# Attention stage of a fused transformer block on one core: the product of the new tokens' values, from one fp32 pass to three fp32r passes with split operands

## The reference

```python
# one sequence: L = 512 cached positions, 32 new ones, 8 key heads, 4 query heads for each
k_all = concat([k_cache[block_table], k], axis=1)      # (544, 8, 128)
v_all = concat([v_cache[block_table], v], axis=1)
scores = einsum('qhd,khd->hqk', q, k_all) * SCALE      # masked behind cache_seqlens
probs = softmax(scores, axis=-1)
o = einsum('hqk,khd->qhd', probs, v_all)               # 512 cached + 32 new positions
out = einsum('se,de->sd', o, Wo)
```

## Time and profile before

| | |
|---|---|
| median of 3 runs | 1250.58 us (1247.67 to 1251.4) |
| profiled execution, its own time | 1247.98 us |
| its span | 1246.0 us |
| busy share of PE, DVE, ACT, POOL | 98%, 63%, 63%, 60% |
| attention of the first and second half | about 160 to 472 us and 780 to 1093 us |

### The profile page before, as it was taken

One profiled execution on the slowest core, in us unless ns is written; L12 is line 12 of the kernel. 1 busy time (PEld: TensorE's weight loads), 2 busy tenths in 40 slices (PEclk: granted clock), 3 DMA queues, 4 the chain that ended last, 5 costly groups with the idle time before them and its releaser, 6 DMA issues.

```text
span 1246.0 us, 28884 instructions
## 1 busy us (share of the span) xinstructions
PE 1221.7 (98%) x7378; PEld 1037.5 (83%) x7378; DVE 782.0 (63%) x1736; ACT 789.6 (63%) x2259; POOL 746.8 (60%) x884
## 2 busy tenths in 40 slices
PE   7999999999999999999999999999999999999998
PEld 6788889999999988865777888889999999988756
DVE  5976666666666668951459666666666666655422
ACT  5666678778877874432345766777887788644320
POOL 5344468888888885433233443788888888744320
PEclk9999999999999999999999999999999999999999
DMA  6524299999999955306135252899999999434300
GB/s 207 194 95 143 98 235 248 235 222 244 234 229 242 232 146 180 142 10 193 68 104 187 85 171 86 236 237 246 228 241 235 229 241 239 109 118 156 90 27 34
DMA packets 147978, 214.82 MB, mean 172 GB/s; under 512 B 24949, under 2 KB 119479, under 8 KB 142136
## 3 DMA queue, kind: packets, MB, share of 16 engines
q1 hardware_dynamic: 123480, 199.62, 58.9%
q10 hardware_dynamic: 24416, 14.28, 4.8%
HBM read 203.33 MB, written 10.49 MB: 172 GB/s over the span
## 4 chain that ended last, share of the span: by engine, by line
PE 91%; DVE 3%; ACT 2%; issue 2%; ACTq 1%; POOL 1%; DMA 0%; DVEq 0%; SPq 0%; POOLq 0%
PE PS L1157 18%; PE PS L1125 9%; PE PS L1224 5%; PE PS L1215 5%; PE PS L1019 5%; PE PS L1221 5%; PE PS L1023 5%; PE PS L1017 5%; PE PS L1167 4%; PE PS L1090 2%; PE PS L1266 2%; PE PS L1108 2%; PE PS L1092 2%; PE PS L1112 2%; PE PS L1102 2%
## 5 line engine op out<-in xcount | busy, mean ns | idle before, releaser
L628 POOL TENSOR_TENSOR kv_parts<-kv,k_hi 128x544 fp32r<-128x544 f32 x192 | 258.1, 1345 | 26.5 <-ACT k_hi L813 26.5
L1157 PE MATMUL PS<-probT,kv 128*128 128x128 f32 x2048 | 270.4, 275 | 0.0
L588 POOL TENSOR_TENSOR ring_parts<-ring,kv_parts 128x512 fp32r<-128x512 f32 x96 | 126.1, 1319 | 209.1 <-ACT kv_parts L691 180.5
L1654 DVE CUSTOM_DVE_ANT_0 ring<-PS,mask,rq 128x544 f32<-128x544 f32 x192 | 150.2, 782 | 158.3 <-PE PS L1113 97.2
L1157 PEld LDWEIGHTS PS<-probT,kv 128*128 128x128 f32 x2048 | 248.9, 192 | 0.0
L870 ACT ACTIVATE ring<-ring,smin 128x544 f32<-128x544 f32 x192 | 143.0, 745 | 97.1 <-DVE smin L1654 94.0
L1665 DVE COPY probT<-PS 128x512 f32<-128x512 f32 x256 | 172.1, 672 | 5.5 <-PE PS L1125 5.5
L650 POOL TENSOR_TENSOR ring_parts<-ring,kv_parts 128x512 fp32r<-128x512 f32 x64 | 84.9, 1330 | 95.3 <-ACT kv_parts L924 95.3
L813 ACT ACTIVATE k_hi<-kv 128x544 fp32r<-128x544 f32 x192 | 124.9, 652 | 16.2 <-DMA kv<-in_kpages 3.9
L616 POOL TENSOR_SCALAR ring<-ring,rinv 128x512 f32<-128x512 f32 x192 | 133.2, 694 | 0.0
L1692 DVE TENSOR_TENSOR qo_parts<-qo,kv_parts 128x512 fp32r<-128x512 f32 x64 | 85.3, 1339 | 54.2 <-ACT kv_parts L932 51.5
(11 more groups left out here) (217 smaller groups left out, 2718.6 us busy)
## 6 DMA issues: line engine op xcount, KB each, us to landing
kv<-in_kpages SPq DMA_DIRECT2D x512, 128.0 KB, 3.3
kv<-in_vpages SPq DMA_DIRECT2D x512, 128.0 KB
ring<-in_w SPq DMA_DIRECT2D x44, 1024.0 KB, 5.1
k_new<-kv ACTq DMA_DIRECT2D x16, 256.0 KB, 2.3
kv<-k_new ACTq DMA_DIRECT2D x28, 128.0 KB, 3.9
kv<-v_new ACTq DMA_DIRECT2D x28, 128.0 KB
kv<-in_xT SPq DMA_DIRECT2D x8, 256.0 KB, 5.3
ring<-in_w SPq DMA_DIRECT2D x8, 256.0 KB, 5.9
```

The source lines that it names most:

```text
L628: nc.gpsimd.tensor_tensor(kbuf_lo(par)[:, :, g, :], kbuf(par)[:, :, g, :], k_hi[:, e % 2, :].rearrange("p (j t) -> p j t", t=PSIZE), ALU.s ...
L1157: mm = nc.tensor.matmul(PS[:, at:at + D], vbuf(bpar)[:, c, gg * D:(gg + 1) * D], probT[:, g % 2, c * P:(c + 1) * P], start=(c == 0 and a = ...
L1654: V.tensor_tensor_reduce(prob(g % PRING)[:, 0:LK], PS[:, at:at + LK], mask[:, par, :], rq[:, par, g:g + 1], 3.0e38, ALU.add, ALU.min, smin ...
```

## The change

`values_new` no longer multiplies `vnew` with `spread` in fp32, but `vnew_hi x spread_hi`, `vnew_lo x spread_hi` and `vnew_hi x spread_lo`, three fp32r matmuls of 512 columns. For that:

- ScalarE's four copies now write fp32r (`spread_hi`), and ScalarE also makes `vnew_hi`, once for each sequence, in its step 4 (5 in the first sequence).
- VectorE makes `spread_lo` with four subtractions of 32x128 (`lower_spread`) at the end of its steps 3 and 7; the third pass and the next turn of new probabilities wait for it.
- GpSimd makes `vnew_lo` (`lower_values`, 128x256) in its step 7, and its low parts of keys move: those of heads 0 and 4 from steps 0 and 4 into the plain head's steps 7 and 3 before them, ahead of the scaling there.
- VectorE takes the reciprocal ahead of the mask instead of behind it in steps 0 and 4, those that follow the subtractions.
- `spread_lo` and `vnew_hi` are new storage, two areas are cleared instead of one.

```diff
-        KVSZ = 18944
+        KVSZ = 19968
...
+                def lower_values(b, par):
+                    pool.wait_ge(vhi_ready, h * HB + b + 1)
+                    nc.gpsimd.tensor_tensor(vnew_lo(par), vnew(par), vnew_hi(par), ALU.subtract).then_inc(vlo_ready, 1)
...
                 def lower_keys(b, par, first, last=False):
+                    if first:
+                        lower_key(b, par, 0)
                     for g in range(HK):
...
-                        if g % GU < NS:
-                            e = g // GU * NS + g % GU
-                            pool.wait_ge(khi_ready, (h * HB + b) * NSB + e + 1)
...
+                        if g % GU == NS and g < HK - 1:
+                            lower_key(b, par, g + 1)
+                        elif g == HK - 1:
+                            lower_values(b, par)
+                            if not last:
+                                lower_key(b + 1, 1 - par, 0)
+                        elif 0 < g % GU < NS:
+                            lower_key(b, par, g)
                         if g >= 2:
                             scale_probs(b, g - 2, first)
...
+                def upper_values(b, par):
...
+                        act.wait_ge(v_in[par], h * (n_in * HB // 2 - less) + (b - par) * (n_in // 2) + n_in - less)
...
+                    nc.scalar.activation(vnew_hi(par), vnew(par), ACT.Copy).then_inc(vhi_ready, 1)
...
+                    if g == (5 if first else 4):
+                        upper_values(b, par)
...
                 def values_new(b, par, u):
+                    if u == 0:
+                        pe.wait_ge(vlo_ready, h * HB + b + 1)
                     pe.wait_ge(spread_ready, GU * (h * QUADS + b * UNITS + u + 1))
-                    nc.tensor.matmul(bank(6 + u), vnew(par)[:, u * D:(u + 1) * D], spread, start=False, stop=True)\
-                        .then_inc(o_done, 1)
+                    nc.tensor.matmul(bank(6 + u), hi, spread_hi, start=False, stop=False)
+                    nc.tensor.matmul(bank(6 + u), lo, spread_hi, start=False, stop=False)
+                    pe.wait_ge(spread_low, GU * (h * QUADS + b * UNITS + u + 1))
+                    nc.tensor.matmul(bank(6 + u), hi, spread_lo, start=False, stop=True).then_inc(o_done, 1)
...
+                def lower_spread(b, u):
+                    dve.wait_ge(spread_ready, GU * (h * QUADS + b * UNITS + u + 1))
+                    for a in range(GU):
+                        rows = slice(a * SEQ, (a + 1) * SEQ)
+                        V.tensor_tensor(spread_lo[rows, a * P:(a + 1) * P], PS[rows, 2560:2688],
+                                        spread_hi[rows, a * P:(a + 1) * P], ALU.subtract).then_inc(spread_low, 1)
...
                 def step(b, par, g, first):
+                    early = g % GU == 0 and g < HK and not (first and g <= GU)
+                    if early:
+                        reciprocal(b, g)
...
-                    if g <= HK and not (first and g == 0):
-                        V.reciprocal(rinv[:, k:k + 1], rsum[:, k:k + 1]).then_inc(rinv_ready, 1)
+                    if g <= HK and not (first and g == 0) and not early:
+                        reciprocal(b, g)
...
+                    if g < HK and g % GU == 3 and not (first and g < GU):
+                        lower_spread(b if g > GU else b - 1, int(g < GU))
```

More of the change, by code:

```diff
@@ L201, in vnew, with vnew_hi, vnew_lo @@
             return kv[:, at:at + UNITS * D]
-        spread = kv[:, 2 * (KSZ + VSZ):2 * (KSZ + VSZ) + GU * P]
+        SP_HI, SP_LO, VN_HI = 2 * (KSZ + VSZ), 18944, 19456
+        spread_hi = kv_parts[:, SP_HI:SP_HI + GU * P]
+        spread_lo = kv_parts[:, SP_LO:SP_LO + GU * P]
+        def vnew_hi(u):
+            return kv_parts[:, VN_HI + u * UNITS * D:VN_HI + (u + 1) * UNITS * D]
+        def vnew_lo(u):
+            at = 2 * KSZ + u * VSZ + 4 * HK * D
+            return kv_parts[:, at:at + UNITS * D]
         junk = [prob0[:, 0:512], probT[:, :, :].rearrange("p a x -> p (a x)")[:, 512:1024]]
@@ L357, in build @@
         spread_ready = sem("spread_ready")
+        spread_low = sem("spread_low")
+        vhi_ready = sem("vhi_ready")
+        vlo_ready = sem("vlo_ready")
         o_done = sem("o_done")
@@ L825, in spread_new @@
                     if isinstance(b, int) and b == 0 and u == 0:
-                        act.wait_ge(spread_clear, h + 1)
+                        act.wait_ge(spread_clear, 2 * h + 2)
                     else:
@@ L831, in spread_new @@
                         rows = slice(a * SEQ, (a + 1) * SEQ)
-                        nc.scalar.activation(spread[rows, a * P:(a + 1) * P], PS[rows, 2560:2688], ACT.Copy)\
+                        nc.scalar.activation(spread_hi[rows, a * P:(a + 1) * P], PS[rows, 2560:2688], ACT.Copy)\
                             .then_inc(spread_ready, 1)
+                def upper_values(b, par):
+                    if isinstance(b, int) and b == 0:
+                        act.wait_ge(first_vnew_in, 16 * (h + 1))
+                    else:
+                        n_in = 16 * (NPP + 1)
+                        less = 16 if par == 0 else 0
+                        act.wait_ge(v_in[par], h * (n_in * HB // 2 - less) + (b - par) * (n_in // 2) + n_in - less)
+                    act.sem_inc(act_past, 1)
+                    nc.scalar.activation(vnew_hi(par), vnew(par), ACT.Copy).then_inc(vhi_ready, 1)
                 def keep_o(b, u):
@@ L1676, in _ @@
                         dve.sem_inc(dve_past, 1)
-                        V.memset(spread, 0.0).then_inc(spread_clear, 1)
+                        V.memset(spread_hi.bitcast(F32), 0.0).then_inc(spread_clear, 1)
+                        V.memset(spread_lo.bitcast(F32), 0.0).then_inc(spread_clear, 1)
                 for g in range(HK):
@@ L1686, in _ @@
                 step(HB - 1, 1, HK + 2, False)
+                lower_spread(HB - 1, 1)
                 def lower(head):
```

30 lines of the change are left out of this document (19 added, 11 removed).

## The result

The changed kernel takes 1253.88 us at the median of its runs (1247.88 to 1262.57) against 1249.58 us (1247.67 to 1261.68) for the kernel before on the same chips: a ratio of 1.0031 with a 95% interval of 1.0019 to 1.0044. It is not faster, and most likely 0.3% slower. The prediction, 1242.5 us, is missed on the wrong side. The profiled execution has a span of 1256.6 us (before: 1246.0); by its own time, 1258.4 us, it lies 4.5 us above the median of the changed kernel's runs, so the trace shows a slower run than most.

A forecast was written before the change was run, and what follows sets the result against it. TensorE, busy 98% of the span, was taken to set the pace, with pages nearly a second bound. Sum: 1247.98 - 10.5 + 0.6 + 3.0 = 1241.1 us, plus 1.3 for the median: 1242.5 us, range 1236.5 to 1247.5.

The forecast's parts named there:

- The product: TensorE's product with the new values: fp32 0.86 us to three fp32r passes of 0.696 us, 64 times, gain 10.5 us.
- VectorE, GpSimd, ScalarE: Added subtractions (0.85 us for four), values' low part (0.75 us) and conversion inside the attention: cost 0 to TensorE.
- the stated margin of 1.5: VectorE, steps after the subtractions: TensorE's next turn is held up only if the four take over 1.5 us.
- End of a half: Last subtractions, with no later step to hide them: 0.3 us lost a half, 0.6 us in all.
- From the profiled execution to the median: Runs' median lies 0 to 2.6 us above the profiled execution; half taken, 1241.1 to 1242.5 us.
- Pages: Key and value loads: first four or five sequences of each half gain nothing, 3 us given back; later 1.5 us to spare.
- pages set the pace throughout: Rival, chance 0.14: backlog of loads never drains, loops of 18.58 to 18.9 us, 1248 us, no measurable change.

The follow-up runs named there:

- e2: Kernel before, with half of each value page left unloaded from the third sequence of a half on: 1248.1 us, ratio 0.9984.
- e1: Changed kernel, with half of each value page left unloaded from the third sequence of a half on: 1239.73 us, ratio 0.9917.
- e13: Changed kernel with half value pages and one fp32 product of the high parts instead of three passes, all added work kept: 1250.32 us.
- e4: Changed kernel with full pages and one fp32 product of the high parts instead of three passes, added work kept: 1253.26 us, ratio 1.0024.
- e15: e4, with VectorE's last four subtractions of each half waiting for ScalarE's copies one by one: 1251.41 us, ratio 1.0008.
- e8: e1, with VectorE's last four subtractions of each half waiting for ScalarE's copies one by one: 1238.55 us.
- e3: Changed kernel, with SyncE reading the next sequence's first 8 page numbers ahead of its wait for v_free: 1253.97 us, ratio 1.0022.
- e5: Changed kernel loading 960 of 1024 columns of each value page from the third sequence of a half on: 1240.28 us, ratio 0.9923.
- e10: Changed kernel loading 992 of 1024 columns of value pages, 1.5% fewer bytes: 1240.87 us, ratio 0.9929.
- e9: Changed kernel loading 1020 of 1024 columns of value pages, 0.2% fewer bytes: 1251.02 us, ratio 1.0015.
- e12: Kernel before, with value and key page loads issued in turn from the tenth value page on: 1261.26 us, ratio 1.0096.
- e14: Kernel before, full pages, with only the storage grown as in the change (KVSZ 19968 instead of 18944): 1249.89 us, ratio 1.0001.
- e18: Kernel before, with each row of a value page described as four pieces of 1 KB: 1249.64 us, ratio 1.0.

## Why the prediction was wrong

- **The product** (0.86 to 0.696 us) was right: 1.74 us against a forecast of 1.72 for the whole stretch, a period of 18.66 us where 18.63 was forecast, and -8.4 us between e2 and e1 with light pages. With the ends' 1.2 us added back that is 9.6 of the 10.5 us forecast.
- **VectorE, GpSimd, ScalarE** were right in their direct effect on TensorE. The four subtractions are 1.23 us, not 0.85, inside the stated margin of 1.5; GpSimd's part is 0.73 for 0.75. e13 shows that they cost TensorE nothing in the loop when pages are light. That they might slow the pages was put at nothing without being named; e4 and e15 suggest it.
- **End of a half**: right mechanism, 0.6 us a half instead of 0.3 (e1 against e8), since the subtractions start only behind the last copy.
- **From the profiled execution to the median** 1.3 us were added. The kernel before has its median 1.6 us above its profiled execution, the changed one 4.5 us below; against a miss of 11 us this is a side matter.
- **Pages: this step failed.** It said that the first sequences of each half would be paced by the pages, "3 us given back", and that "later the new period leaves 1.5 us to spare". Both terms were too small. The first four intervals of the two halves lost 9.2 us in the profiled execution, not 3, and the later ones 10.0, not 0. The 1.9 us to spare were read off SyncE's queue, which is idle that long between two groups of loads. But that is the issuing queue's time, not the DMA engines'. Their share stood beside it: 0.93 to 0.96 over 19 us, and 0.95 to 0.99 over windows of 80 us. Taken as time these are 17.7 to 18.8 us; of a new period of 18.66 us they leave 1.0 us at best, and at worst nothing. e3 shows that issuing sooner gains nothing, e1, e5 and e10 that lighter loads of pages give back nearly all.
- **The rival "pages set the pace throughout"** had the right mechanism ("the backlog never drains") and the wrong price. It assumed that pages only stretch the period, up to 18.9, so that the time could never come out above before's. In fact the delay is invisible for some sequences, while landings climb, and is then paid in an interval that is 0.6 to 4.2 us too long, in three places partly at the lower clock. On average over a half the loads then start 19.3 and 19.4 us apart, further than in the kernel before (19.1 and 19.0).
- **Left open**: why the pages come in time every 18.97 us and not every 18.66, what in the DMA engines or behind them sets this limit, and how much of it is the added work (e15 is 1.5 us above before, within its interval). It wasn't tried to spread the loads over other queues, or to keep TensorE busy during a stall so that its clock holds.

## What to carry to other kernels

When an engine is made faster, ask what share of the new period each other resource needs, and for the DMA engines look at their own share and at the trend of the landings, not at the idle time of the queue that issues. Here a share of 0.95 to 0.99 of the old period left no room for a period 1.7% shorter. A stream that is a little too slow needn't cost a little: here it drifted until a stall, and three of the stalls were paid again in clock. A cheap test is to cut the suspected bytes by a few per cent and to see whether the lost time comes back at once. Such a cut changes the size of the transfers too, so it names the resource and not its margin. And test the added work with the load as heavy as it really is: with light pages (e13) it looked free.

## What the runs showed of the hardware

- TensorE's granted clock fell to 0.53 right after three short waits of together 1.87 us within 3.2 us, none longer than 0.99 us; behind waits of 0.98 and 0.24 us elsewhere in the same trace it stayed at 1.00.
- The DMA engines' busy share at the same 239 GB/s was 0.94 with value rows of 3968 bytes (e10) and 1.00 with 4096 (changed kernel); since 4080 bytes (e9, 0.94 to 1.01 over windows of 80 us) behave nearly like 4096, it isn't the round size. Over such windows e10 has 0.90 to 0.93, the kernel before 0.95 to 0.99.
- Alternating loads of rows of 1 KB and of 4 KB in one queue made even the kernel before 12 us slower (e12), with TensorE waiting 8.1 us for value pages and no ScalarE wait for keys.
- Four operations on 32x128 from PSUM take 1.23 us on VectorE, 0.31 from one start to the next, though each is recorded with 0.285 us.
- At the same period (18.98 us) and with the same bytes the longest landing of key pages was at most 5.3 us in the later part of a half in the kernels without the added work (before, e14, e18), and up to 7.1 us in those with it (e4, e15).
